# Loads of x in slices and stores of y on GpSimd's queue in the down projection of a Trainium2 adaLN block

## The reference, cut to what matters

```python
mod = (silu(c) @ wmod).reshape(8, 6, 1, -1)
sa, ca, ga, sb, cb, gb = (mod[:, i] for i in range(6))
ga, gb = (sign(g) * maximum(abs(g), 0.25) for g in (ga, gb))   # sign(0) = +1
h = layernorm(x) * (1 + ca) + sa
x = x + ga * local_attention(h, Wq, Wk, Wv, Wo)     # window 512, 16 heads, 4 kv heads
h = layernorm(x) * (1 + cb) + sb
gate = silu((h @ fp8(gate_w)) * gate_scale)
up = (h @ fp8(up_w)) * up_scale
x = x + gb * (((gate * up) @ fp8(down_w)) * down_scale)
```

## Time and profile before

| | us |
|---|---|
| median of three timed runs | 4770.3 |
| the three timed runs | 4412.6, 4770.3, 4883.1 |
| the profiled execution | 4417.6 |
| its span, slowest core (core 1) | 4416.0 |
| spans of the eight cores | 4382.6 to 4416.0 |
| granted TensorE clock, the eight cores | 0.859 to 0.866 |
| busy: PE, PEld, DVE, ACT, POOL | 3308.5, 1547.8, 809.4, 772.7, 406.6 |
| matmuls of gate, up and down (L818, L828, L888), busy | 704.7, 694.4, 708.9 |

### The profile page before, as it was taken

How to read it: one execution, slowest core, us unless ns; L and a number is a source line. 1 busy time by engine, 2 the same in 40 slices (tenths; PEclk the granted TensorE clock), 3 DMA queues, 4 the chain that set the end, 5 groups by cost and what they waited for, 6 DMA issues and landing times.

```text
span 4416.0 us, 48731 instructions; the slowest of 8 cores (4382.6 to 4416.0 us)
## 1 busy us (share of the span) xinstructions
PE 3308.5 (75%) x16778; PEld 1547.8 (35%) x16778; DVE 809.4 (18%) x1682; ACT 772.7 (17%) x1329; POOL 406.6 (9%) x536
## 2 busy tenths in 40 slices
PE   3433029996666669979987599977599987599877
PEld 0000014443344434434443244433244433244433
DVE  0001232005555540031100211101211100311010
ACT  0000240115555551120000020000110000200000
POOL 1001000014444441000000000000000000000000
PEclk7565559998888889979998789989699988699988
DMA  6767741359999996122222212231222222222321
GB/s 123 127 124 122 127 101 15 39 50 107 105 106 106 110 111 81 41 74 77 77 103 76 88 58 77 77 107 64 77 77 77 96 84 69 72 77 76 112 66 65
DMA packets 476586, 377.75 MB, mean 86 GB/s; under 512 B 384160, under 2 KB 386912, under 8 KB 469952
## 3 DMA queue, kind: packets, MB, share of 16 engines
q0 software_dynamic: 362688, 148.10, 32.4%
q1 hardware_dynamic: 113664, 226.53, 15.7%
HBM read 505.40 MB, written 62.96 MB: 129 GB/s over the span
## 4 chain that ended last, share of the span: by engine, by line
PE 69%; DMA 14%; issue 7%; DVE 5%; ACT 3%; another core or an unknown queue 1%; DVEq 0%; SPq 0%; ACTq 0%; POOLq 0%; POOL 0%
PE PSf L888 16%; PE PSf L818 15%; PE PSf L828 14%; DMA wmodb<-wmod 6%; PE PSf L651 5%; PE PSf L498 5%; DMA y<-x3p 3%; PE PSf L551 2%; PE PSf L534 2%; DMA d<-d_scr 2%; PE PSf L565 2%; PE PSf L310 2%; DMA s_xe<-x 2%; PE PSf L538 1%
## 5 line engine op out<-in xcount | busy, mean ns | idle before, releaser
L888 PE MATMUL PSf<-fuse,d 128*128 128x512 bf16 x3072 | 708.9, 393 | 229.8 <-DMA d<-d_scr 229.8
L818 PE MATMUL PSf<-h,g 128*128 128x512 bf16 x3072 | 704.7, 383 | 4.5 <-ACT h L790 4.5
L828 PE MATMUL PSf<-h,u8w 128*128 128x512 bf16 x3072 | 694.4, 379 | 0.0
L888 PEld LDWEIGHTS PSf<-fuse,d 128*128 128x128 fp8e4 x3072 | 306.3, 101 | 609.1 <-issue 281.6
L818 PEld LDWEIGHTS PSf<-h,g 128*128 128x128 fp8e4 x3072 | 302.9, 99 | 374.7 <-issue 19.2
L828 PEld LDWEIGHTS PSf<-h,u8w 128*128 128x128 fp8e4 x3072 | 300.6, 98 | 362.5
L845 DVE SCALAR_TENSOR_TENSOR fuse<-PSf,gsus,sy 128x512 bf16<-128x512 f32 x192 | 144.2, 751 | 1255.4 <-ACT sy L840 1255.4
L840 ACT ACTIVATE sy<-PSf,gsus 128x512 bf16<-128x512 f32 x192 | 132.0, 687 | 1164.2 <-PE PSf L828 1164.2
L310 PE MATMUL PSf<-wmodb,csi 128*1 128x512 bf16 x384 | 164.9, 597 | 222.6 <-DMA wmodb<-wmod 210.3
L534 PE MATMUL PSf<-k_fm,q_fm 128*128 128x512 bf16 x256 | 115.8, 452 | 209.0 <-ACT s_p L599 203.2
L574 DVE TENSOR_REDUCE negmax<-PSf 128x1 f32<-128x640 f32 x256 | 209.0, 816 | 223.0 <-PE PSf L540 222.8
(11 more groups left out here) (103 smaller groups left out, 2175.3 us busy)
## 6 DMA issues: line engine op xcount, KB each, us to landing
wmodb<-wmod POOLq DMA_DIRECT2D x64, 768.0 KB, 7.7
g<-g_scr SPq DMA_DIRECT2D x192, 256.0 KB, 2.8
u8w<-u_scr SPq DMA_DIRECT2D x192, 256.0 KB, 3.0
d<-d_scr SPq DMA_DIRECT2D x64, 768.0 KB, 5.0
s_x<-x SPq DMA_DIRECT2D x16, 1024.0 KB, 4.8
s_u<-x SPq DMA_DIRECT2D x16, 1024.0 KB, 4.9
s_xe<-x SPq DMA_DIRECT2D x16, 1024.0 KB, 4.9
y<-x3p SPq DMA_DIRECT2D x64, 256.0 KB, 2.4
```

Source lines behind the costliest of these rows:

```text
L818: ev("pe", lambda e, par=par, kc=kc: e.matmul(bankf(0 + par), g8[:, par, :].rearrange("p (c n) -> p c n", c=16)[:, kc, :].bitcast(F8), h2[ ...
L828: ev("pe", lambda e, par=par, kc=kc: e.matmul(bankf(2 + par), u8w[:, par, :].rearrange("p (c n) -> p c n", c=16)[:, kc, :].bitcast(F8), h2 ...
L888: ev("pe", lambda e, par=par, m=m_, dbk=dbk: e.matmul(bankf(dbk), d8[:, par, :].rearrange("p (a n) -> p a n", a=NM)[:, m, :].bitcast(F8), ...
```

## The change

The loads of `x` for the residual leave SyncE. They become slices of 128 tokens by 512 features, four for each `dcg`, issued by GpSimd into a new buffer `s_xe2` with two slots for `dcg`, which lies over `h2`. The slices for the first two `dcg` wait for the last product of `fuse` (`FUSEQ`), the others for the adds of the `dcg` two before. The stores of `y` are issued by GpSimd too; `x3p` has four slots, one for each `t4`, and each slot has its own store semaphore. Order on GpSimd's queue in a quarter: slices 0, slices 1, stores 0, slices 2, stores 1, slices 3, stores 2, stores 3. The arithmetic is the same.

```diff
-    x3p = sb("x3p", [128, 2, 512], F32)
+    x3p = sb("x3p", [128, 4, 512], F32)
...
-    s_xe = sb("s_xe", [128, 4, D], F32, off=O_KV)
...
+    s_xe2 = sb("s_xe2", [128, 4, 2, 512], F32, off=O_A + 49152)
...
+    dOL = [C("dO0", 16), C("dO1", 16), C("dO2", 16), C("dO3", 16)]
...
-        for t4 in range(4):
-            tc = Q * 4 + t4
-            ev("sy", lambda e, tc=tc, t4=t4: e.dma_start(
-                s_xe[:, t4, :], xin[tc * 128:(tc + 1) * 128, :]),
-               sc=dXE,
-               waits=[(c_vxh, XH4), (c_tr, c_tr.n), (c_fve, epi_done),
-                      (c_sq, c_sq.n)])
-        XE_OK = dXE.n
...
+        def emit_xe(dcg):
+            guard = FUSEQ if dcg < 2 else epi_add_after[dcg - 2]
+            for t4 in range(4):
+                tc = Q * 4 + t4
+                ev("gp", lambda e, tc=tc, t4=t4, dcg=dcg: e.dma_start(
+                    s_xe2[:, t4, dcg % 2, :],
+                    xin[tc * 128:(tc + 1) * 128, dcg * 512:(dcg + 1) * 512]),
+                   sc=dXE, waits=([(c_fve, guard)] if t4 == 0 else []))
+            xe_cnt[dcg] = dXE.n
...
-                pp = (dcg * 4 + t4) % 2
-                pidx = Q * 16 + dcg * 4 + t4
-                ev("ve", lambda e, t4=t4, dcg=dcg, pp=pp: e.tensor_tensor(
-                    x3p[:, pp, :], s_xe[:, t4, dcg * 512:(dcg + 1) * 512],
+                g = Q * 4 + dcg
+                ev("ve", lambda e, t4=t4, dcg=dcg: e.tensor_tensor(
+                    x3p[:, t4, :], s_xe2[:, t4, dcg % 2, :],
                     bankf(4 + t4), ALU.add),
                    inc=c_fve,
-                   waits=[(c_tr, TRG), (dXE, XE_OK),
-                          (dO, 16 * (pidx - 1))])
+                   waits=[(c_tr, TRG), (dXE, xe_cnt[dcg]),
+                          (dOL[t4], 16 * g)])
                 brel(4 + t4, c_fve)
-                ev("sy", lambda e, tc=tc, dcg=dcg, pp=pp: e.dma_start(
+                ev("gp", lambda e, tc=tc, dcg=dcg, t4=t4: e.dma_start(
                     yout[tc * 128:(tc + 1) * 128,
-                         dcg * 512:(dcg + 1) * 512], x3p[:, pp, :]),
-                   sc=dO, waits=[(c_fve, c_fve.n)])
-
+                         dcg * 512:(dcg + 1) * 512], x3p[:, t4, :]),
+                   sc=dOL[t4], waits=[(c_fve, c_fve.n)])
+            epi_add_after[dcg] = c_fve.n
...
         for dc in range(NCD + 1):
             if dc < NCD:
+                if dc % 4 == 0:
+                    emit_xe(dc // 4)
                 emit_downmm(dc)
```

More of the change, by code:

```diff
@@ L928, in emit_epilogue @@
                 tc = Q * 4 + t4
-                pp = (dcg * 4 + t4) % 2
-                pidx = Q * 16 + dcg * 4 + t4
-                ev("ve", lambda e, t4=t4, dcg=dcg, pp=pp: e.tensor_tensor(
-                    x3p[:, pp, :], s_xe[:, t4, dcg * 512:(dcg + 1) * 512],
+                g = Q * 4 + dcg
+                ev("ve", lambda e, t4=t4, dcg=dcg: e.tensor_tensor(
+                    x3p[:, t4, :], s_xe2[:, t4, dcg % 2, :],
                     bankf(4 + t4), ALU.add),
                    inc=c_fve,
-                   waits=[(c_tr, TRG), (dXE, XE_OK),
-                          (dO, 16 * (pidx - 1))])
+                   waits=[(c_tr, TRG), (dXE, xe_cnt[dcg]),
+                          (dOL[t4], 16 * g)])
                 brel(4 + t4, c_fve)
-                ev("sy", lambda e, tc=tc, dcg=dcg, pp=pp: e.dma_start(
+                ev("gp", lambda e, tc=tc, dcg=dcg, t4=t4: e.dma_start(
                     yout[tc * 128:(tc + 1) * 128,
-                         dcg * 512:(dcg + 1) * 512], x3p[:, pp, :]),
-                   sc=dO, waits=[(c_fve, c_fve.n)])
+                         dcg * 512:(dcg + 1) * 512], x3p[:, t4, :]),
+                   sc=dOL[t4], waits=[(c_fve, c_fve.n)])
+            epi_add_after[dcg] = c_fve.n
+        xe_cnt = {}
+        epi_add_after = {}
         for dc in range(NCD + 1):
             if dc < NCD:
+                if dc % 4 == 0:
+                    emit_xe(dc // 4)
                 emit_downmm(dc)
@@ L952, in build @@
         epi_done = c_fve.n
-    NOUT = dO.n
-    ev("sy", lambda e: e.nop(), waits=[(dO, NOUT)])
-    ev("gp", lambda e: e.nop(), waits=[(dO, NOUT)])
+    drain = [(s, s.n) for s in dOL] + [(dO, dO.n)]
+    ev("sy", lambda e: e.nop(), waits=drain)
+    ev("gp", lambda e: e.nop(), waits=drain)
     for name in DBG:
```

## The result

The changed kernel is faster: 0.933 of the time before (95% interval 0.932 to 0.935). Ten runs have a median of 4123.4 us (4116.6 to 4490.5), ten of the kernel before 4534.8 (4409.3 to 4883.1). The profiled execution took 4116.7 us with a span of 4115.1; the forecast was 4114 and 4112. Some executions of either kernel run with the cores of one die at a lower granted clock, two of the first three of the kernel before among them, and the ratio and all that follows leave these out: what remains is 4409 to 4421 before and 4117 to 4124 after.

A forecast was written before the change was run, and what follows sets the result against it. Bound: TensorE, idle in the down projection while d8 loads stand behind other transfers on SyncE's queue. Gains 260 + 39.2 + 4.5 = 304; 4417.6 - 304 = 4114 us; own range 4099 to 4140, overall 4090 to 4190.

The forecast's parts named there:

- Parts 1 and 2: Down projection: of 229.8 us of waits for d8 loads, four of 1.9 us for fuse stay; 222.2 us go.
- Part 4: Between two quarters: adds stop waiting for y stores and s_u loads start earlier; gain 39.2 us.
- Part 5: Program's end: the last adds follow each other without waiting for stores; gain 4.5 us.
- Part 6: Other edits: arrays behind x3p move by 4 KB, GpSimd issues 128 DMAs; claimed to cost nothing.
- Part 3: Down projection: chunks slowed by a fallen clock after the d8 waits return to 10.36 us; gain 38.4 us.
- rival A: Down projection: stores collide with d8 loads, 12 come late; 24 to 76 us lost, 4138 to 4190; chance 0.12.
- rival B: Epilogues: slices of x come late on GpSimd's queue and TensorE stops; 144 us, 4258; chance 0.05.
- C: Feed-forward matmuls: granted clock falls with TensorE busier; all gain gone at 13%, slower by 2% from 16%; chance 0.06.
- D: SyncE's queue: the change saves only issue time of 64 stores and 16 loads, 27 us, 4391; chance 0.02.

The follow-up runs named there:

- the last kernel on SyncE alone: Changed kernel with all transfers on SyncE, next d8 load first, slices on four semaphores, two s_u loads ahead of the last epilogue's stores: ratio 0.933.
- the first one on SyncE alone: Changed kernel with all transfers back on SyncE, the next chunk's d8 load ahead of slices and stores: 4146.0 and 4149.1 us, ratio 0.940.

## Where the prediction was right, and the step that failed

**Where its steps held.** Parts 1 and 2: 221.7 us, forecast 222.2; the waits that stay are 2.0 us, forecast 1.9. Part 4: by its own terms, the waits of VectorE, 12.9 + 28.7 - 3.1 = 38.5, and by the crossings' length 37.8; forecast 39.2. Part 5: 8.4 us from the last epilogue's first add to the end, forecast about 8, gain 4.0 against 4.5. Part 6: no cost was seen.

**Part 3** forecast 38.4 and added that some would stay if the clock fell in the short wait too. It did, in one quarter of four. Windows of the changed kernel: a gate and up, then the 10 us just after the wait, in the first quarter and in the last (length, PE busy, granted clock, DMA share, GB/s):

```profile
3047.00:3360.00 313.00, 311.47 (x1423) 1.00 0.23 76
2262.20:2272.20 10.00, 9.91 (x46) 1.00 0.18 54
3934.20:3944.20 10.00, 9.87 (x38) 0.83 0.22 54
```

The last down projection takes 172.2 us to the end of its transposes, the others 170.5: 1.7 us came back. The same wait of 2.0 us left the clock at its upper level, 2.4 GHz, in the three others. The restarts gave 36.3 us, forecast 38.4.

**The step that failed** is the base. The prediction made its sum against the profiled execution of 4417.6 us, named the stated median of 4770.3 as 353 us above it, and gave these 353 us no term: the forecast is "for an execution like it". Against the profiled execution 4114 us is a gain of 6.9%, against the stated median one of 13.8%; measured are 6.7%. A reader who takes 4114 as a statement on the stated 4770.3 expects twice what the change does. What the runs show in its place: the times of the kernel before that are compared are 4409 to 4421, within 0.3% of its profiled execution, and the gain on them is some 293 us, not 656. The 353 us were no part of what the change acts on, and the forecast should have been given as a ratio to the profiled execution: 4114 / 4417.6 = 0.931, against 0.933 measured.

Two sizes inside the hidden parts were wrong. Slices were put at 2.4 us and took 3.9; the flight of stores was put at 2.4 and, for four at once, 3.2, and its median is 4.4:

```profile
s_xe<-x POOLq DMA_DIRECT2D x64, 256.0 KB, 3.9
y<-x3p POOLq DMA_DIRECT2D x64, 256.0 KB, 4.4
```

They cost nothing here, as eight slices had 53 us for the first four and 95 for all. Only the program's last four stores, with nothing beside them, landed after 2.5 to 3.1 us, near the 3.2 of part 5.

Three pieces of the working don't come out, though the forecast doesn't hang on them. Its own range has 15 us for the slowest core either way, but its upper bound of 4140 holds only the other 26.5 us. In rival A, 12 loads at 2 to 3 us with 1.5 to 3 us of restart are 42 to 72 us, not 24 to 76. In rival B the later slices do not have 42.3 us: those of `dcg` 2 wait for the adds of `dcg` 0 and are read eight chunks later, after 84.6 us. In the trace the first of them is issued at 2876.39 and the adds that read them begin at 2957.37.

**The rivals.** A: the collision lengthens the flight of `d8`, from a longest of 8.2 us to 8.9, and even 9.3 with the stores doubled, but never past a chunk; only the kernel with slices alone, in which the load is exposed, paid for it clearly. B: slices at 3.9 us are far from being late; no wait for `s_xe2` was seen. C: the granted clock in gate and up is 1.00, as before (the first row above). D: refuted by the result. The Trainium skill's rule on which it leaned (DMA: Bandwidth & Descriptors, section Issuing engines are not separate DMA queues) is borne out in its own terms, for the kernel that uses SyncE alone is as fast; but it speaks of the time to start a transfer, and what stood in this queue was waiting.

## What to carry to other kernels

A wait on a queue costs what stands behind it: look in the timeline at which transfers sit between a slot that came free and its refill, before asking how long any transfer takes. A semaphore shared by all transfers of a kind chains them, and buffers laid over each other chain what has no data in common; separate them first, and then either reorder the one queue or use a second, which here came to the same. Give a forecast as a ratio to the profiled execution where the timed runs spread.

## What the runs showed of the hardware that was not expected

A 256 KB store costs a little more from GpSimd than from SyncE. The cleanest rows are the program's last four stores, with nothing else in flight: chained one by one they land 2.7 us after issue from GpSimd and 2.4 from SyncE (the kernel before); four at once, 2.5 to 3.1 from GpSimd (the changed kernel) and 2.4 to 2.6 from SyncE (the last kernel on SyncE alone). An issue occupies GpSimd for 0.54 us, SyncE for 0.33. The first store leaves GpSimd 0.6 us after its add has ended (adds from 2989.98, 0.69 us each, first store at 2991.29); in the kernel before SyncE's left within 0.2 (last adds from 4403.64, first store at 4404.45).

The flight of transfers in company moved more than the engine that issued them explains. In the changed kernel the 16 stores with no load beside them took a median of 3.0 us, the 48 others 4.9; in the kernel with chained stores on GpSimd it is 2.7 for the 26 alone and 3.7 for the 38 others. Over all 64, stores in groups of four took a median of 4.4 us in the changed kernel and 3.3 with the stores alone on GpSimd, 4.7 and 3.0 in the two kernels that use SyncE alone. What flies beside them differs between these, and no run here separates the amount from the kind.

Whether a pause of 2.0 us of TensorE brings its clock down varied within one execution and from one to the next. By the granted clock of the 10 us behind each of the four pauses, 0.83 where it fell and 1.00 where not: once in four in the changed kernel, in the kernel with slices alone and in the first one on SyncE alone, three times in the second one on SyncE alone, in all four with every store twice, and never with chained stores. Each fall cost some 1.7 us. No run here shows what decides it.
